# Graph attention on one core: DVE turns the mask bytes of every second unit in the last two chunks, by turns with PE

## The reference

```python
h  = maximum(layernorm(x), 0)                 # no scale, no shift
Wh = h @ W
e  = (Wh @ a[:F])[:, None] + (Wh @ a[F:])[None, :]
e  = where(e > 0, e, 0.2 * e)
e  = where(adj > 0, e, -9e15)
out = x + elu(softmax(e, axis=1) @ Wh)
```

## Time and profile before

| | us |
|---|---|
| time, median of 3 runs (lowest to highest) | 244.91 (244.35 to 244.97) |
| the profiled execution's own time | 244.79 |
| its span, first to last instruction | 243.0 |
| PE busy | 227.0 (93%) |
| DVE busy | 196.4 (81%) |
| ACT busy | 156.2 (64%) |
| POOL busy | 59.1 (24%) |
| `adj` and `x` read from HBM | 69.27 MB |

### The profile page before, as it was taken

One profiled execution on the slowest core, in us unless ns is written; L12 is line 12 of the kernel. 1 busy time (PEld: TensorE's weight loads), 2 busy tenths in 40 slices (PEclk: granted clock), 3 DMA queues, 4 the chain that ended last, 5 costly groups with the idle time before them and its releaser, 6 DMA issues.

```text
span 243.0 us, 8254 instructions
## 1 busy us (share of the span) xinstructions
PE 227.0 (93%) x3736; PEld 221.2 (91%) x3736; DVE 196.4 (81%) x259; ACT 156.2 (64%) x139; POOL 59.1 (24%) x48
## 2 busy tenths in 40 slices
PE   6969999599999999999999999999999999999970
PEld 2759899599998999999999999999999999999970
DVE  4999997536776998889887988898879888998864
ACT  3698836697799999944996677019975774000051
POOL 3648036897000070300000560000001710040000
PEclk9997999999999999999999999999999999999995
DMA  6999999999998999999999999999999300020002
GB/s 225 360 389 386 386 386 385 388 367 370 301 352 284 363 395 386 388 385 385 398 386 385 388 385 385 385 387 369 386 386 386 140 0 3 3 89 3 3 0 92
DMA packets 36521, 71.92 MB, mean 296 GB/s; under 512 B 1282, under 2 KB 1924, under 8 KB 36484
## 3 DMA queue, kind: packets, MB, share of 16 engines
q1 hardware_dynamic: 35520, 69.74, 79.0%
q10 hardware_dynamic: 964, 1.64, 1.8%
HBM read 69.27 MB, written 2.10 MB: 294 GB/s over the span
## 4 chain that ended last, share of the span: by engine, by line
PE 74%; ACT 8%; DVE 7%; issue 4%; POOL 4%; DMA 1%; ACTq 0%; DVEq 0%; POOLq 0%
PE acc L834 20%; PE acc L835 20%; PE acc L836 20%; PE mask_t L817 11%; ACT mask L420 4%; POOL v L330 2%; POOL val L333 2%; ACT neg L432 1%; DVE words L610 1%; DVE stats L547 1%; DMA x_sb<-in_x_dram 1%; PE acc L796 1%; PE acc L805 1%; ACT neg L511 1%; DVE wh_sb L573 1%
## 5 line engine op out<-in xcount | busy, mean ns | idle before, releaser
L610 DVE SCALAR_TENSOR_TENSOR words<-g_row,gq_word,mask_t 128x1024 f32<-128x1024 f32 x128 | 161.4, 1278 | 36.0 <-PE acc L836 19.0
L834 PE MATMUL acc<-val,words 128*128 128x129 f16 x1000 | 171.9, 220 | 0.3 <-DVE wh_sb L573 0.3
L835 PE MATMUL acc<-val,words 128*128 128x129 f16 x1000 | 171.9, 220 | 0.0
L836 PE MATMUL acc<-val,words 128*128 128x129 f16 x1000 | 171.9, 220 | 0.0
L420 ACT ACTIVATE mask<-raw,step_bias 128x2048 uint8<-128x2048 int32 x63 | 121.8, 1993 | 28.4 <-DVE x_sb L626 17.3
L834 PEld LDWEIGHTS acc<-val,words 128*128 128x128 f16 x1000 | 97.8, 98 | 0.5 <-issue 0.5
L835 PEld LDWEIGHTS acc<-val,words 128*128 128x128 f16 x1000 | 97.9, 98 | 0.1
L836 PEld LDWEIGHTS acc<-val,words 128*128 128x128 f16 x1000 | 97.8, 98 | 0.0
L817 PE MATMUL mask_t<-ident_b,mask 128*128 128x128 bf16 x512 | 34.3, 221 | 1.8 <-ACT mask L420 1.8
L817 PEld LDWEIGHTS mask_t<-ident_b,mask 128*128 128x128 bf16 x512 | 30.3, 99 | 2.2 <-ACT mask L420 2.2
L358 POOL TENSOR_TENSOR hp<-num,rz 128x1024 f32<-128x1024 f32 x3 | 5.7, 1897 | 105.3 <-DVE rz L621 105.3
(11 more groups left out here) (91 smaller groups left out, 125.4 us busy)
## 6 DMA issues: line engine op xcount, KB each, us to landing
raw<-in_adj_dram SPq DMA_DIRECT2D x64, 1024.0 KB, 14.1
x_sb<-in_x_dram SPq DMA_DIRECT2D x8, 256.0 KB, 5.7
out_dram<-x_sb ACTq DMA_DIRECT2D x3, 512.0 KB, 7.9
out_dram<-x_sb SPq DMA_DIRECT2D x2, 128.0 KB, 2.4
out_dram<-x_sb SPq DMA_DIRECT2D x1, 192.0 KB, 1.9
w_sb<-in_L_gnn_W_dram ACTq DMA_DIRECT2D x1, 64.0 KB
out_dram<-x_sb SPq DMA_DIRECT2D x1, 64.0 KB, 1.6
a_sb<-in_L_gnn_a_dram ACTq DMA_DIRECT2D x1, 1.0 KB
```

Of the source, the lines that this page charges most:

```text
L610: nc.vector.scalar_tensor_tensor(words[:, q], g_row[:, c * CHUNK:(c + 1) * CHUNK], gq_word[:, 1, t:t + 1], maskt_bytes[:, u % 2, q // 2, : ...
L834: nc.tensor.matmul(acc_tile(t), high, val[:, tile, 0, 0:V], start=first and t % PT == 0, stop=False, skip_group_check=True)
L835: nc.tensor.matmul(acc_tile(t), high, val[:, tile, 1, 0:V], start=False, stop=False, skip_group_check=True)
L836: last = nc.tensor.matmul(acc_tile(t), low, val[:, tile, 0, 0:V], start=False, stop=False, skip_group_check=True)
```

## The change

It touches chunks 2 and 3 (`SETS = 2`), the end of each chunk from the second on, and the layout of memory.

- The units of chunks 2 and 3 are taken in the order 0, 4, 1, 5, 2, 6, 3, 7. Units 4 to 7 are "sets": their bytes are turned by DVE, units 0 to 3 by PE as before. `turn_set` is one DVE transpose in squares of 32x32 of 128x1024 four-byte elements, from SBUF into the same PSUM buffer, and stands ahead of `weights` of q = 3 of the unit before.
- A square of 32 stays within 32 partitions, so the four sets of a chunk are loaded in another shape: load h (of four) brings 256 rows x 2048 columns, in four DMAs of 512 KB, each to 32 partitions; SP issues those to partitions 0 to 63 and ACT, in its own queue (`load_set`), those to 64 to 127. All four loads must be there, and converted (`set_to_bytes`), before the first set can be turned. Loads are in the order set 0, set 1, unit 0, set 2, set 3, units 1, 2, 3. The masks go to other buffers (`pairs`).
- The neighbours of a set lie in another order, so the upper half of `val` and of the words is copied once into that order by 16 small DMAs of SP (`move_values`), and `x` of chunks 2 and 3 is read again, row by row as they now lie (`load_rows`).
- `take_sums(1)` and `take_sums(2)` go from DVE to ACT (three copies out of PSUM); POOL adds the seed, DVE keeps the reciprocal (`invert`). `result` goes from DVE to POOL. In `tail`, ACT takes the negative part and POOL the positive.
- The last output goes in three DMAs, by bank, where there were four.

```diff
+    ORDER = [[*range(U)] if c < SETS else [0, 4, 1, 5, 2, 6, 3, 7] for c in range(C)]
+    LOADS = [(c, u, None) for c in range(SETS) for u in range(U)]
+    for c in range(SETS, C):
+        LOADS += [(c, None, 0), (c, None, 1), (c, 0, None), (c, None, 2), (c, None, 3), (c, 1, None), (c, 2, None), (c, 3, None)]
...
+            def load_set(at):                                   # SP; ACT has the same for k = 2, 3
+                c, _, h = LOADS[at]
+                for k in SP_QUARTERS:
+                    sp.dma_start(raw[k * QUARTER:(k + 1) * QUARTER, at % RING], adj_set[c, 1, h, k]).then_inc(set_in[at % RING], 16)
...
+            for at in range(U, C * U):                          # ACT
+                c, u, h = LOADS[at]
+                if u is None:
+                    set_to_bytes(c, h)
+                else:
                     for k in range(2):
                         to_bytes(c, u, k)
+                load_set(at + RING)
+                if at == 13:
+                    tail(0)
+                if at == 15:
+                    store(0)
+                if at == 19:
+                    take_sums(1)
+                if at == 22:
+                    tail(1)
+                if at == 26:
+                    store(1)
+                if at == 28:
+                    take_sums(2)
+            tail(2)
+            store(2)
...
+            def take_sums(c):                                   # ACT
+                if c >= 2:
+                    act.wait_ge(hp_ready, c + 1)
+                for k, (t0, t1) in enumerate(BANKS):
+                    wait_bank(act, c, k)
+                    nc.scalar.copy(num[:, t0:t1], acc_bank(k)).then_inc(acc_free, 1)
...
+            def turn_set(c, i):                                 # DVE
+                m = ORDER[c][i] - 4
+                if m == 0:
+                    dve.wait_ge(act_bytes, 2 * LOADS.index((c, None, 3)) + 1)
+                dve.wait_ge(words_ready, 4 * (c * U + i - 1))
+                nc.vector.transpose(maskt_quads[:, i % 2].rearrange("p (t h r) -> p t h r", h=4, r=QUARTER),
+                                    pair_quads[PAIRS[c][m // 2]][:, m % 2]).then_inc(set_turned, 1)
...
                 for u in range(U):
                     for q in range(BT):
+                        if q == BT - 1 and u < U - 1 and is_set(c, ORDER[c][u + 1]):
+                            turn_set(c, u + 1)
                         weights(c, u, q)
-                        if (u, q) == (0, 2):
-                            take_sums(c - 1)
-                        if (u, q) == (4, 3):
-                            result(c - 1)
+                        if c == 1 and (u, q) == (0, 2):
+                            take_sums(0)
+                        if c >= 2 and (u, q) == (1, 1):
+                            invert(c - 1)
...
+            def turn_ahead(c, i):                               # PE
+                if i == U - 1:
+                    c, i = c + 1, -1
+                if not is_set(c, ORDER[c][i + 1]):
+                    turn(c, i + 1)
```

More of the change, by code:

```diff
@@ L37 @@
 RING = 4
+QUARTER = 32
 WORDS = 4
@@ L258, in _ @@
                 load_x(b)
[L259 to L275, removed]
+            for at in range(1, C * U):
+                if LOADS[at][1] is None:
+                    sp.wait_ge(act_bytes, 2 * (at - RING) + 1)
+                    load_set(at)
+                else:
+                    for k in range(2):
+                        if (at, k) == (RING, 0):
+                            sp.wait_ge(first_bytes, 1)
+                        elif at >= RING:
+                            sp.wait_ge(act_bytes, 2 * (at - RING) + (1 if LOADS[at - RING][1] is None else k))
+                        load_raw(at, k)
+                if 18 <= at < 22:
+                    if at == 18:
+                        sp.wait_ge(vl_ready, G - 1)
+                        sp.wait_ge(pad_ready, 2)
+                        sp.wait_ge(ht_ps, NB)
+                    move_values(at - 18)
+                if at == 26:
+                    sp.wait_ge(words_free, SETS * U * BT)
+                    sp.wait_ge(val_moved, MOVES * 16)
+                    load_rows(C - 2)
+                    load_rows(C - 1)
+            last = out_lin[C - 1].rearrange("p (t f) -> p t f", f=F)
+            for k, (t0, t1) in enumerate(BANKS):
+                sp.wait_ge(last_res, k + 1)
+                sp.dma_start(last[:, t0:t1], rows_of(C - 1)[:, t0:t1]).then_inc(out_done, 16)
             sp.wait_ge(general_ready, 1)
@@ L414, in to_bytes @@
             def to_bytes(c, u, k):
[L415 to L420, removed]
-                                     scale=1.0, bias=step_bias[:, 0:1]).then_inc(act_bytes, 1)
+                at = LOADS.index((c, u, None))
@@ L833, in product @@
                     low = words_h[:, q, t * P:(t + 1) * P, LO]
-                    nc.tensor.matmul(acc_tile(t), high, val[:, tile, 0, 0:V], start=first and t % PT == 0, stop=False, skip_group_check=True)
-                    nc.tensor.matmul(acc_tile(t), high, val[:, tile, 1, 0:V], start=False, stop=False, skip_group_check=True)
-                    last = nc.tensor.matmul(acc_tile(t), low, val[:, tile, 0, 0:V], start=False, stop=False, skip_group_check=True)
-                    if (u, q) == (U - 1, BT - 1) and t in (2, 5):
+                    nc.tensor.matmul(acc_tile(t), high, v[:, 0, 0:V], start=first and t % PT == 0, stop=False, skip_group_check=True)
+                    nc.tensor.matmul(acc_tile(t), high, v[:, 1, 0:V], start=False, stop=False, skip_group_check=True)
+                    last = nc.tensor.matmul(acc_tile(t), low, v[:, 0, 0:V], start=False, stop=False, skip_group_check=True)
+                    if (i, q) == (U - 1, BT - 1) and t in (2, 5):
                         last.then_inc(acc_done, 1)
@@ L906, in _ @@
                 if u == U - 1:
-                    turn(0, u + 1)
+                    turn_ahead(0, u)
                 for q in range(BT):
@@ L930, in _ @@
                     else:
-                        turn(c, u + 1)
+                        turn_ahead(c, u)
                         for q in range(BT):
```

203 lines of the change are left out of this document (152 added, 51 removed).

## The result

The changed kernel takes **287.2 us** (285.1 to 287.8, 4 runs) against 244.7 us for the kernel before beside it: a ratio of 1.172 (95% interval 1.166 to 1.179). The prediction said 242.8 us, range 237.5 to 252.0, and was wrong: 42.5 us slower, not 2 us faster. The profiled execution took 286.8 us, its span is 285.0 us.

The account below looks back on a forecast made before the run. PE was taken as the bound, the loads nearly a second. Terms -7.24 + 3.1 + 0.7 + 1.0 + 0.6 + 0.2 - 0.5 = -2.1 us gave 240.9 + 1.8 + 0.1 = 242.8 us, range 237.5 to 252.0.

Parts of the forecast that it names:

- with D = 5.43: Loads of the sets: each takes 5.43 us, so load 20 lands at 130.0 us and load 28 at 177.5 us.
- 4.9 us to spare: Second border, before unit 24: load 28 converted at 181.4 us, needed by 186.3 us, so no stop there.
- the case: Rival, set loads too slow: load 28 late if a set load exceeds 6.0 us; 247.2 or 253.7 us; chance 0.25.
- near 280 us: Set loads by the skill's port rule, kept apart from the sum: some 11 us per set load, time near 280 us.
- about 2: Load stream before load 20: the moved values, 1.3 MB in all, add about 2 us to its landing.
- Turns spared: PE in chunks 2 and 3: eight of 32 units no longer turned, 8 x 0.905 = 7.24 us saved.
- DVE is the bound: Rival, unit pairs: at 2.2 us per transpose a pair takes 12.2 us against 11.77; 247.2 us; chance 0.07.
- The first border and its clock: Unit 16: ACT's sums delay load 20, PE dry +3.1 us, load 21 late +0.7, half clock +1.0 net.
- load 21 at 144.1: First border: ACT converts load 21 by 144.1 us after two DMA issues; PE wants it at 143.4, +0.7 us.
- Startup +0.2: Kernel start: two DVE copies of 0.18 us, one of them where DVE is always busy, +0.2 us.
- The end: Last output: with one DMA fewer SP issues the last at about 239.6 us, not 240.14: -0.5 us.
- +0.6 at the last unit: Unit 31: DVE needs 7.4 us for transpose and words, PE is through its first product at 6.79: +0.6 us.

Follow-up runs that it names:

- a_wide_moves: Changed kernel with set loads to all 128 partitions and values copied by four 128-partition DMAs instead of sixteen 32-partition ones (output not the reference's): 243.2 us, ratio 0.993.
- b_last_act: Kernel before, with the third of the four last output DMAs issued by ACT instead of SP: 244.4 us against 244.9, ratio 0.998.
- b_step_sp: Kernel before, eight of its 32 loads each as four 512 KB DMAs to every fourth partition, all from SP: 244.8 us, single run.
- b_block_sp: Kernel before, eight of its 32 loads each as four 512 KB DMAs to 32 adjacent partitions, all from SP: 266.7 us, single run.
- b_block64: Kernel before, eight loads each as two 1 MB DMAs to partitions 0 to 63 and 64 to 127, from SP: 272.1 us, single run.
- b_block_alt: Kernel before, eight loads each as eight 256 KB DMAs to 32 adjacent partitions, alternating between partition halves, all from SP: 258.6 us, single run.
- one_b: Changed kernel with sets in the last chunk only, units ordered 0, 1, 4, 2, 5, 3, 6, 7, sums of chunk 1 behind load 20: 276.3 us.
- b_block_two: Kernel before, eight loads each as four 512 KB DMAs to 32 adjacent partitions, partitions 64 to 127 from ACT's queue: 258.1 us, single run.

## Why the prediction was wrong, step by step

- **The step that failed: the landing of the set loads**, "with D = 5.43" (D is the time that one set load takes), and with it "4.9 us to spare" at the second border. D was read from a row of 128-partition loads, for a form that the trace did not have. In windows with narrow loads alone it is 9.9 us from one queue. In the changed kernel load 28 is converted at 229.9 us, with wide set loads at 195.9, so each of the eight set loads costs 34.0 / 8 = 4.25 us more than 5.43: D = 9.7. I had named the case as a rival, found its threshold (6.0 us, 10% above 5.43), and then bounded it by the two slowest rates that the trace happened to hold, 318 and 282 GB/s, neither of which had to do with the place of partitions. The chance of 0.25 was too small, and the range's end at 252.0 left the case out.
- **The sentence on the Trainium skill's port rule**, "near 280 us", came nearest. It is right in its cause and partly lucky in its size: its D was 11 us, and it had nothing for the copies or for late landings.
- **The copies**, "about 2" us of stream for 1.3 MB: load 28 is converted at 195.9 us with them and at 187.8 with wide ones, 8.1 us, and the time is 9.6 us longer (252.8 against 243.2). That the place of their partitions is the cause is likely, not shown.
- **The landings with every DMA wide**: load 28 is converted at 187.8 us, not 181.4. So the 48.5 us between 181.4 and 229.9 are 6.4 of this, 8.1 of the copies and 34.0 of the narrow form. The four set conversions ran from 180.1 to 187.8 us in one piece: load 27 was ready at 180.1 us (forecast 172.1) and load 28 at 183.9 at the latest. I had put them 5.43 us apart, one behind the other, with half of each in ACT's queue. Loads 19 and 20 show the same. So the "4.9 us to spare" were not there even with wide loads, and removing the first border's stop bought no time.
- **Turns spared**, 7.24 us: right. In the changed kernel a pair of units takes 11.78 us (251.41 to 263.19 us on DVE below), as forecast, against 12.67 before.

```profile
251.41 3.93 DVE L793 SCALAR_TENSOR_TENSOR words<-g_row,gq_word,mask_t 128x1024 f32<-128x1024 f32 x3 [0.76 <-PE acc L1025]
255.26 1.25 DVE L773 STREAM_TRANSPOSE mask_t<-second 128x1024 uint32<-128x1024 uint32 x1
...
263.19 3.93 DVE L793 SCALAR_TENSOR_TENSOR words<-g_row,gq_word,mask_t 128x1024 f32<-128x1024 f32 x3 [0.75 <-PE acc L1025]
```

- **DVE's transpose**, 1.25 us: 1.25 us, and DVE waits 0.76 us in each pair. The rival "DVE is the bound" is out (its terms add up to 247.0, not 247.2). Eight times the 311 ns of the Trainium skill, "VectorE: DVE Perf Modes", section on the three transpose paths, is 2.5 us, twice what was measured for this shape and type.
- **The first border and its clock**: right in place and in the order of events, too small in size (6.8 us by `a_wide_moves`, against 4.8), and only in part what it was said to be. Taking the sums away from ACT wins 4.1 of it. Two errors hide each other in "load 21 at 144.1": the sums were done 0.6 us earlier than forecast, and ACT's two issues took 1.3 us, not 0.84.
- **242.8 against 243.2** in `a_wide_moves` is partly luck. The border cost 2.0 us more than forecast; the stage up to the first sums took 0.4 us less than before, not 0.2 more; the end took 0.9 us less, not 0.5. These misses leave 1.0 us, close to the 0.8 us between its span of 241.7 and the forecast 240.9.
- **Small terms.** Startup +0.2: the first sums come at 84.13 us in the changed kernel, 83.65 in `a_wide_moves` and 84.09 before, so a term of this size is not told apart from the difference between two executions. The end, from DVE's last word to the end of the span: 11.8 us before, 10.8 after, -1.0 and not -0.5; `b_last_act` says that the earlier issue is not the reason. The +0.6 at the last unit can be had by difference only: from the first sums to the last word `a_wide_moves` takes 147.2 us, the kernel before 147.1; with 7.24 spared and 6.8 lost, some 0.5 us remain.

## What to carry to other kernels

- A DMA to a block of adjacent partitions is not a DMA to all 128, whatever its size: before a layout is built on it, time it by itself in the old kernel. Here that took one short edit and cost 22 us from one queue and 14 from two, of the 42.
- Where the stream of loads has little to spare, its rate is the first term to bound, not the last. Here 10% on one term used up all the spare time, and no row gave that term.
- A sum that comes out right is no proof of its terms. Hold each against the trace; here an error of 2.0 us in one was hidden by smaller ones.
- A rival's price must come from the worst row of the same mechanism. If there is none, the range has to reach as far as the arithmetic of the mechanism does.

## What the runs showed of the hardware that I had not expected

- 32 partitions 4 apart load at 384 to 397 GB/s but for two slices (`b_step_sp`), 32 adjacent ones at 211 (`b_block_sp`, 130 to 145 us), 64 adjacent ones no faster (`b_block64`, 202 in 100 to 120 us).
- Pieces that alternate between the halves in one queue raise 211 GB/s to 246, not to 386 (`b_block_alt`). Two queues bring as much time back (266.7 to 258.1 us, against 258.6), in single runs.
- The DMA engines' busy share is 1.08 at 176 GB/s (`one_b`) and 1.05 at 388 (`a_wide_moves`): the share doesn't tell a slow stream from a full one, GB/s does.
- DMAs in ACT's queue are served beside those that SP issued before. Load 15, a plain one that SP had issued by 90.2 us, is ready in full at 109.8 us in the changed kernel and 110.1 in `b_block_two`, where ACT issued halves of narrow loads from 92.7 us on; with SP alone as the issuer it is ready at 106.0 (`b_block_sp`).
- DVE turns 128x1024 four-byte elements in squares of 32, from SBUF to PSUM, in 1.25 us, the price of one pass over them (1.22 us for a scalar_tensor_tensor of that size).
